# Four staging banks and another gate order in the last feed-forward; maxima split on GpSimd in two cross-attentions

## The reference

```python
def _L2_xattn_ref(...):                       # third cross-attention, L2X
    logits = einsum('bhqd,bhkd->bhqk', q, k) / sqrt(DEPTH)
    logits = logits + mask[None, None, :, :] * -1000000000.0
    weights = softmax(logits, axis=-1)        # 77 keys, 16 heads
    attn = einsum('bhqk,bhkd->bhqd', weights, v)
...
def _L3_xattn_ref(...):                       # fourth, L3X
    scores = einsum('bhqd,bhkd->bhqk', q, k) * inv_scale
    scores = where(mask[:, None, :, :] == 0, min_val, scores)
    attn = softmax(scores, axis=-1)
    ctx = einsum('bhqk,bhkd->bhqd', attn, v)
...
def _inl(ctrl, xs, vs, mu):
    a, b, g = split(ctrl, 3, axis=-1)
    v_next = sigmoid(a) * vs - softplus(b) * (xs - mu)
    return xs + DT * sigmoid(g) * v_next, v_next
def _L3_ffn_ref(...):                         # last feed-forward, L3F
    probs = softmax(_gelu(xf @ router_w1 + router_b1) @ router_w2 + router_b2)
    topk_p, topk_i = top_k(probs, 2)          # of 8 experts
    topk_p = topk_p / sum(topk_p)
    v, integrated = zeros_like(xf), xf
    for _ in range(2):
        ctx = concatenate([integrated, v], axis=-1)
        shared_ctrl = _gelu(ctx @ shared_w1 + shared_b1) @ shared_w2 + shared_b2
        x_sh, v_sh = _inl(shared_ctrl, integrated, v, mu)
        ctrl = ...                            # both chosen experts' gelu layers
        x_r, v_r = ...                        # _inl of each, weighted by topk_p, added
        x_next = sw * x_sh + (1.0 - sw) * x_r
        v_next = sw * v_sh + (1.0 - sw) * v_r
        halt = sigmoid(_gelu(integrated @ halt_w1 + halt_b1) @ halt_w2 + halt_b2)
        integrated = integrated + halt * (x_next - integrated)
        v = v + halt * (v_next - v)
    refined = _gelu(integrated @ refine_w1 + refine_b1) @ refine_w2 + refine_b2
    return xf + integration_weight * refined
```

## Time and profile before

| | before |
|---|---|
| median of 3 runs | 5264.44 us (5246.1 to 5288.91) |
| the profiled execution's own time | 5250.1 us |
| its span in the trace | 5248.4 us |
| busy share PE / PEld / DVE / ACT / POOL | 84% / 45% / 51% / 36% / 18% |
| TensorE clock granted, mean of full speed | 0.89 |

### The profile page before, as it was taken

The page is one execution under the profiler, slowest core; times in us unless marked ns, Lnnn a source line. Parts: engine busy times, 40 slices in busy tenths (PEclk is TensorE's granted clock), DMA queues, the critical chain, the costliest instruction groups (busy, mean ns, idle before and its releaser), DMA issues. The chain is left out here.

```text
span 5248.4 us, 63414 instructions
## 1 busy us (share of the span) xinstructions
PE 4404.1 (84%) x23432; PEld 2353.8 (45%) x23432; DVE 2698.8 (51%) x6209; ACT 1905.3 (36%) x3352; POOL 920.5 (18%) x804
## 2 busy tenths in 40 slices
PE   6898889888689888988868988898886898889887
PEld 3454444633435444463344544446334454444632
DVE  6555443643656544364365554436436555443743
ACT  3243222445324322344532432224453243222445
POOL 2121100222202110022221211002222021100222
PEclk8898899989789889987978988998897898899989
DMA  2000100000100010000010001000001000100000
GB/s 79 1 3 27 58 5 2 17 2 2 54 0 3 27 58 5 2 17 1 2 54 0 3 27 58 5 2 17 2 2 54 0 3 27 58 5 2 17 1 4
DMA packets 20900, 93.01 MB, mean 18 GB/s; under 512 B 5228, under 2 KB 14444, under 8 KB 17796
## 3 DMA queue, kind: packets, MB, share of 16 engines
q1 hardware_dynamic: 20580, 88.80, 4.5%
HBM read 86.70 MB, written 2.10 MB: 17 GB/s over the span
## 5 line engine op out<-in xcount | busy, mean ns | idle before, releaser
L217 POOL TENSOR_SCALAR rstd_e<-mean_var 128x4 f32<-128x4 f32 x120 | 27.3, 228 | 2497.2 <-DVE mean_var L183 2496.7
L2167 DVE TENSOR_TENSOR arena<-ps,arena 128x512 f32<-128x512 f32 x256 | 176.5, 691 | 464.4 <-ACT arena L2117 464.4
L2117 ACT ACTIVATE arena<-ps 128x512 f32<-128x512 f32 x288 | 172.0, 597 | 603.5 <-PE ps L2065 603.4
L1625 ACT ACTIVATE arena<-ps 77x512 f32<-77x512 f32 x384 | 196.4, 591 | 458.6 <-PE ps L1543 458.6
L2507 PE MATMUL ps<-w_even,w_odd 128*128 128x512 f32 x640 | 325.1, 655 | 26.9 <-issue 26.9
L2064 PE MATMUL ps<-xT,w_even 128*128 128x512 f32 x576 | 306.1, 613 | 3.1 <-DVE arena L2154 3.1
L2071 PE MATMUL ps<-arena,w_even 128*128 128x512 f32 x576 | 295.0, 594 | 7.0 <-DVE arena L2167 4.7
L766 PE MATMUL ps<-xT,w_even 128*128 128x512 f32 (+1 forms) x544 | 269.4, 618 | 0.4
L2065 PE MATMUL ps<-arena,w_even 128*128 128x512 f32 x512 | 264.4, 598 | 0.0
L206 DVE TENSOR_TENSOR y_tok<-ps,x_tok 128x512 f32<-128x512 f32 x72 | 49.4, 686 | 343.0 <-PE ps L704 265.4
L1803 PE MATMUL ps<-arena,w_odd 128*128 128x512 f32 x512 | 220.4, 592 | 0.0
(11 more groups left out here) (431 smaller groups left out, 9503.4 us busy)
## 6 DMA issues: line engine op xcount, KB each, us to landing
w_even<-in_w SPq DMA_DIRECT2D x4, 6916.0 KB, 19.0
w_even<-in_w SPq DMA_DIRECT2D x4, 3313.5 KB, 10.7
w_odd<-in_w SPq DMA_DIRECT2D x4, 2824.5 KB, 9.6
w_odd<-in_w SPq DMA_DIRECT2D x4, 2095.0 KB, 8.3
w_odd<-in_w SPq DMA_DIRECT2D x4, 2048.0 KB, 15.0
x_in<-in_x SPq DMA_DIRECT2D x10, 256.0 KB, 2.9
w_odd<-in_w SPq DMA_DIRECT2D x4, 577.0 KB, 4.1
result<-x_tok SPq DMA_DIRECT2D x8, 256.0 KB, 2.3
```

What stands on the lines that cost most here:

```text
L1625: nc.scalar.activation(m["PT"][j % 2][:, c, :], bank(2 + c)[0:KC, :], ACT.Exp, scale=scale)\
L2117: nc.scalar.activation(e_sg[i % 2], bank(i % 2), ACT.Silu).then_inc(e_silu.sem, 1)
L2167: j = nc.vector.tensor_tensor(e_h[i % 2], bank(2 + i % 2), e_sg[i % 2], ALU.mult)
```

## The change

There are three parts. The first is in the cross-attentions L2X and L3X: the five instructions that split the maxima go from DVE to POOL, on a new signal `k_maxima` that DVE releases after a turn's last maximum. DVE waits, before the first maxima of a turn j, until the split of turn j - 2 is done. POOL takes the split of a turn before the queries of the next one; in L2X its two bias additions go behind the splits of turns 3 and 5 (they were ahead of the queries of turns 0 and 2). L1X stays as it was.

The second part, in L3F, gives the first 42 items (router to the last spread) four banks in turn, 6, 7, 0, 3, where they had 6 and 7; the router's logits go to banks 1 and 4, which were 0 and 3. Of the 26 copies of turned choices and spreads DVE takes 12 (turned 1 and the even spreads), ACT keeps 14. DVE does its setup in another order.

The third part, in L3F too, moves ACT's halt(2) and halt(3) behind the gate functions that followed them, and refine(0) on ACT and PE behind gates(3, 2).

```diff
+        k_rm = signal("k_maxima", [(L, j) for L in (L2X, L3X) for j in J])
...
+        def max_parts(engine, m, j):
+
+            mx = m["mx"][j % 2].rearrange("p (c r) -> p c r", r=4)
+            rest = m["rest"].rearrange("p (c r) -> p c r", r=4)
+            m3 = m["m3"][j % 2].rearrange("p (c s) -> p c s", s=32)
+            engine.tensor_copy(m3[:, :, 0:4], mx)
+            engine.drain()
+            engine.tensor_tensor(rest, mx, m3[:, :, 0:4], ALU.subtract)
+            engine.drain()
+            engine.tensor_copy(m3[:, :, 4:8], rest)
+            engine.drain()
+            engine.tensor_tensor(rest, rest, m3[:, :, 4:8], ALU.subtract)
+            engine.drain()
+            return engine.tensor_copy(m3[:, :, 8:12], rest)
...
+                    if L != L1X and p == 0 and j >= 2:
+                        dve.wait_ge(k_m3.sem, k_m3[L, j - 2])
...
+                    if p == 1 and L != L1X:
+                        nc.vector.drain().then_inc(k_rm.sem, 1)
...
-                        split_max(i)
+                        if L == L1X:
+                            split_max(i)
...
+                    pool_context_queries(pool, L, 0)
+                    pool_context_queries(pool, L, 1)
+                    for j in J:
+                        split_max(j)
+                        if 2 <= j + 1 < 8:
+                            pool_context_queries(pool, L, j + 1)
+                        if L == L2X and j in (3, 5):
+                            pool_add_bias(pool, L, PREV[L], (j - 3) // 2, W(L, "bo"))
...
+        BY_DVE = ([("turned", g, 1) for g in G] + [("spread", g, n) for g in G for n in range(0, 10, 2)])
...
+        for n, item in enumerate(ITEMS):
+            k = (6, 7, 0, 3)[n % 4] if n <= ITEMS.index(("spread", 1, 9)) else 6 + n % 2
+            i_bank[item], i_bank_user[item], last_user[k] = k, last_user.get(k), item
...
-                if i_staged[item] > 2:
-                    pe.wait_ge(i_taken.sem, i_staged[item] - 2)
-                return bank(staged_bank(item))
+                if i_bank_user[item]:
+                    wait_taken(pe, i_bank_user[item])
+                return bank(i_bank[item])
...
             gates(3, 0)
             gates(3, 1)
+            gates(3, 2)
             refine(0)
-            gates(3, 2)
             pe.wait_ge(sub_read.sem, sub_read[L3F, 0])
             refine(1)
...
-                for k in range(3):
+                for k in (0, 2):
...
-                for n in range(10):
+                for n in range(1, 10, 2):
...
             gates(1, 1)
+            gates(1, 2)
             halt(2)
-            gates(1, 2)
             gates(2, 0)
             hidden(3)
             gates(2, 1)
+            gates(2, 2)
             halt(3)
-            gates(2, 2)
             gates(3, 0)
-            refine(0)
             gates(3, 1)
             gates(3, 2)
+            refine(0)
             refine(1)
...
+            def take_spread(g):
+
+                dve.wait_ge(i_staged.sem, i_staged["turned", g, 1])
+                nc.vector.tensor_copy(i_sT[g][1], bank(i_bank["turned", g, 1])[0:24, 0:T // 2].bitcast(BF16))\
+                    .then_inc(i_spread_taken.sem, 1)
+                for n in range(0, 10, 2):
+                    dve.wait_ge(i_staged.sem, i_staged["spread", g, n])
+                    nc.vector.tensor_copy(i_w[g][n] if n < 2 else i_mb[g][n - 2], bank(i_bank["spread", g, n]))\
+                        .then_inc(i_spread_taken.sem, 1)
+
+            split_biases()
             for g in G:
                 less_max(g)
-            select(0)
-            to_mean(0)
-            split_biases()
-            select(1)
-            to_mean(1)
+            for g in G:
+                select(g)
+            for g in G:
+                to_mean(g)
+            for g in G:
+                take_spread(g)
+            nc.vector.drain()
```

More of the change, by code:

```diff
@@ L1739, in pool_context, with split_max @@
         def pool_context(L):
+            m = CB[L]
             def run(pool):
[L1742 to L1745, removed]
+                def split_max(j):
+                    pool.wait_ge(k_rm.sem, k_rm[L, j])
+                    if j >= 2:
+                        pool.wait_ge(k_mt.sem, k_mt[L, j - 2])
+                    max_parts(nc.gpsimd, m, j).then_inc(k_m3.sem, 1)
+                if L == L1X:
+                    for j in J:
+                        if j in (0, 2):
+                            pool_add_bias(pool, L, PREV[L], j // 2, W(L, "bo"))
+                        pool_context_queries(pool, L, j)
+                else:
+                    pool_context_queries(pool, L, 0)
+                    pool_context_queries(pool, L, 1)
+                    for j in J:
+                        split_max(j)
[3 more added lines that the diff above has]
+                            pool_add_bias(pool, L, PREV[L], (j - 3) // 2, W(L, "bo"))
                 for g in G:
@@ L2417, in build @@
         i_logit = signal("i_logits", list(G))
+        BY_DVE = ([("turned", g, 1) for g in G] + [("spread", g, n) for g in G for n in range(0, 10, 2)])
         i_staged = signal("i_products_staged", ITEMS)
-        i_taken = signal("i_staged_taken", ITEMS)
+        i_taken = signal("i_staged_taken", [i for i in ITEMS if i not in BY_DVE])
+        i_spread_taken = signal("i_spread_taken", [("turned", 0, 1)] + [("spread", 0, n) for n in range(0, 10, 2)]
+                                + [("turned", 1, 1)] + [("spread", 1, n) for n in range(0, 10, 2)])
+        i_bank, i_bank_user, last_user = {}, {}, {}
+        for n, item in enumerate(ITEMS):
+            k = (6, 7, 0, 3)[n % 4] if n <= ITEMS.index(("spread", 1, 9)) else 6 + n % 2
+            i_bank[item], i_bank_user[item], last_user[k] = k, last_user.get(k), item
         GATES = [(q, m) for q in range(12) for m in ((1, 2, 0) if q >= 6 else (1, 2))]
@@ L2477, in spread @@
                     mm.then_inc(i_staged.sem, 1)
-                pe.wait_ge(i_taken.sem, i_taken["turned", g, 2])
+                wait_taken(pe, ("turned", g, 1))
+                wait_taken(pe, ("turned", g, 2))
                 for n in range(10):
@@ L2570, in take @@
                 act.wait_ge(i_staged.sem, i_staged[item])
-                nc.scalar.activation(out, bank(staged_bank(item))[0:rows, :], f, **kw).then_inc(i_taken.sem, 1)
+                nc.scalar.activation(out, bank(i_bank[item])[0:rows, :], f, **kw).then_inc(i_taken.sem, 1)
             def hidden(s):
```

31 lines of the change are left out of this document (12 added, 19 removed).

## The result

The changed kernel takes 5122.8 us in the median of four runs (5095.45 to 5132.93); the kernel before took 5255.27 in four runs on the same chip. The ratio is 0.974, with a 95% interval of 0.9711 to 0.9768. The forecast was 5134 (5085 to 5195), 116 us less than before; 132 us less came.

| stretch | forecast, a step | measured, mean of four steps |
|---|---|---|
| hidden layers' end to gate (0,1), the layers themselves, products of gate (0,1) | 7.5 | 5.2 + 0.0 + 0.6 = 5.8 |
| wait behind halt(2), with its products | 4.0 | 4.1 |
| wait behind halt(3), with its products | 6.4 | 6.8 |
| refine(0), with refine(1)'s products | 6.1 | 6.2 + 1.5 = 7.7 |
| L2X, first scores to last heads | 5 | 8.3 |

What follows compares the result with a forecast made beforehand. Time was to come only from stretches where PE idles or runs at its lower clock. 7.5 + 4.0 + 6.4 + 6.1 + 5 + 0 = 29 a step, 116 in four, from 5250 to 5134; range 5085 to 5195.

Steps and rivals of the forecast that it cites:

- The steps on halt(2), halt(3) and refine(0): L3F: moving halt(2) gains 4.0 a step, halt(3) 6.4, and refine(0), moved into PE's idle before refine(1), 6.1.
- the step that left it at the low clock: L3F: refine(1) stays at 3.48 us, so 6.1 a step is gained; at the high clock 1.98, gaining 7.6.
- The price: L2X and L3X: a split on POOL takes 1.75 us, five instructions at 0.23 and four gaps of 0.15.
- The two paths to the turn: L2X: the reciprocal's path ends at about 668.5, POOL's at 668.7; the turn comes 0.65 earlier in six turns.
- both halves: L2X: earlier turns gain 2.5 a step net; mask products gain 2.5 of a possible 6.3 with the clock.
- the hidden layers lose the wait for two banks: L3F hidden layers: 24 instructions would take 10.8 instead of 13.80; 0 to 3.0 gained, 1.2 taken.
- ACT's copies pace it: L3F spreads in the kernel before: ACT's copies set the pace, two taking 1.06 us.
- the step that had the two takers carry the gain: L3F spreads: with ACT and DVE copying side by side, two groups gain 3.2 at 1.2 GHz, 9.6 at 2.4 GHz.
- B: Rival, chance 0.17: the clock stays up wherever a wait goes; 40.8 a step, 163 in all, 5087.
- D: Rival, chance 0.12: only low ends; TensorE bounds spreads at 1.2 GHz, refine(0) runs slow; 15.9 a step, 5186.
- C: Rival, chance 0.13: POOL's split takes as long as the wait it replaces; net 34.8 - 16 x Tp, 5162 or 5250.
- E: Rival, chance 0.08: POOL takes about 1.04 for each split instruction, 5.8 a split; -34 a step, 5386.

Runs made afterwards that it cites:

- the swap of the spreads: The changed kernel with the second group's spreads on PE ahead of the shared gate instead of behind it; 5132.12 us, ratio 0.9772.
- the doubled split: The changed kernel with POOL's five instructions of the split done twice; 5275.69 us, ratio 1.005 to the kernel before.

## Why the prediction was right, point by point

**Gates and refine.** The steps on halt(2), halt(3) and refine(0) came out within 0.4 us, since each was read as a wait whose cause ACT's order gave, and both halves, the wait and the products behind it, had a row. refine(1) took the high end given for it (1.98 instead of 3.48): the step that left it at the low clock was too careful by 1.5. Over all stretches the sum was 5 a step short, 20 us in four. That the median still lies within 11 us of the forecast is in part luck, since the forecast counts from one execution of 5250 and executions of the changed kernel lie up to 37 us apart.

**Split on POOL.** The price was right: a split takes 1.59 where 1.75 was taken, 0.196 to 0.221 an instruction, and the lower row, L217, was the one to be near. The Trainium skill, "GPSIMD Engine Reference", section "Engine selection", has GpSimd about twice as slow for two-input operations; for 16 values the measured subtraction is 0.22 against DVE's 0.18, and there the measurement decides. The two paths to the turn end together, as worked out, and the wait is 0.82 where 1.0 was expected. What was mis-sized in L2X is both halves, each taken at 2.5 a step. Six turns wait 0.8 to 0.95 less and the first two 0.4 to 0.5 more, 4.2 in all; the clock behind them gave the other 4.0. Together 8.3 came, near the upper end of 8.8. The products are short in most turns now.

**The spreads.** The sum was near (5.8 against 7.5), part of its reasoning wrong. The step "the hidden layers lose the wait for two banks" failed: nothing was gained there. The window of the kernel before, which the prediction did not read, shows it:

```profile
1126.96:1132.00 5.04, 5.04 (x8) 2.08 (x8) 3.88 (x31) 2.89 (x4) 0.00 (x0) 0.53 0.00 0
1132.00:1140.76 8.76, 8.76 (x20) 2.09 (x18) 7.33 (x34) 6.17 (x9) 0.00 (x0) 1.00 0.00 0
```

PE is busy for all of the 13.80, for the first 5.04 us at a clock of 0.53: most of what lies above 10.8 is TensorE's own time at the low clock, and hardly any of it a wait for a bank. Two more terms were off. A spread takes 0.43 to 0.45, and not the 0.52 that was half of a pair's 1.03. And "ACT's copies pace it" was half the truth: a pair's copies take 1.08, but a pair came every 1.29 us, since PE and ACT waited 0.20 and 0.21 for each other in turn, as the timelines of the kernel before show:

```profile
1147.40 1.09 PE L2485 MATMUL ps<-arena,expand 8*128 8x512 bf16 x2 [0.20 <-ACT arena L2571]
...
1148.04 1.08 ACT L2571 ACTIVATE arena<-ps 128x512 bf16<-128x512 f32 x2 [0.21 <-PE ps L2485]
```

So the step that had the two takers carry the gain was wrong in its cause: with two banks the sharing gives nothing, with four it gives 1.0 of 5.2. What four banks removed is that handover from ACT back to PE after each pair.

**The rivals.** B (the clock stays up) was right in L2X, at gates and refine(1), and wrong in the spreads, which stay at 0.50. D's picture of the spreads (TensorE-bound at 1.2 GHz) is the one that the trace and the swap of the spreads show. C and E did not come, but their arithmetic was tested: for the doubled split, 3.29, C's formula gives 34.8 - 16 x 3.29 = -17.8 a step, with L3F's 24 still 25 us faster than before in all; it was 23 us slower. The formula priced waits alone; what a longer wait does to the clock behind it, in L3X above all, it left out. By a straight line between the two measured points (the changed kernel's 0.974 at 1.6 us a split, 1.005 at some 3.3), the gain is used up at about 3.0, which is an estimate.

**What the text did not foresee** is that the first two turns of L3X can now run slow; the last section has it.

## What to carry to other kernels

A wait on TensorE had two prices in this kernel, its own length and the slow products behind it; both stand in the rows, and the second was from a fifth (refine) to a half (L2X) of the whole. Before moving small work to a slower engine, find its shortest row for an operation of that size and the end of the path that it joins: here POOL could take 1.6 us because DVE's path to the same turn ended at that moment, and twice that would have cost more than everything gained. When two engines seem to share a load, separate the buffers from the hands: most of the gain came from two more banks, and the second copying engine added little.

## What was not expected of the hardware

The same instructions, with hardly a wait among them, run at either clock from one step to the next. L3X's first turns in the changed kernel, by the windows view, in the first and in the second step (14.0 and 11.0 us of it):

```profile
1053.00:1067.00 14.00, 13.63 (x50) 4.54 (x50) 3.97 (x8) 2.64 (x5) 2.22 (x7) 0.51 0.00 1
2334.00:2345.00 11.00, 9.86 (x55) 3.61 (x56) 3.98 (x8) 2.64 (x5) 2.22 (x7) 0.89 0.00 0
```

In the first, PE is busy for 13.63 of 14.00 and still has 0.51 of its clock; in the second it is granted 0.89. Two turns take 9.7 and 9.7 in the one and 7.4 and 8.0 in the other, 5 us a step. In the eight profiled executions with L3X's split on POOL (the doubled one left out) such first turns came in 16 of 32 steps, in some executions in none and in others in all four; in the four with L3X's split on DVE they came in none of 16, though other turns ran slow there in some. All 16 fall in the six executions with L1X's split on DVE (16 of 24); in the two with it on POOL there is none in 8. L1X's last turns do the same in some steps (8.2 and 9.2 instead of 5.6 and 5.5). Such turns would account for most of the 0.5% by which executions of one kernel differ, which no run here tested, and they are why L3X's own share of the change can't be told. What sets the clock in a stretch in which PE hardly waits is left open.

One more thing bears on the price of the split on DVE, which the prediction did not read. In the kernel before, the five instructions take 1.17 us in an undisturbed turn, but 1.6 to 2.0 in most turns of L3X and up to 2.66 in L1X. All 61 instructions among them that take over 0.25 us end 0.03 us after one of POOL's that spread the queries (L1462), as here in L3X (timelines of POOL and DVE):

```profile
1077.73 1.04 POOL L1462 TENSOR_TENSOR w_even<-arena,const 128x512 f32<-128x512 f32 x1 [6.34 <-PE ps L1543]
...
1078.21 0.60 DVE L1682 CAST arena<-arena 128x16 bf16<-128x16 f32 x1
```

The cast takes 0.60 where it takes 0.17 alone. On POOL, which does both in turn, the split takes 1.58, at most 1.88. So in L3X POOL is hardly the slower place for it, and what the two engines do at the same moment belongs in such a comparison.
